# Self-attention's first query half masked by VectorE on the way out of the score banks, in a new order of work

## What is computed

```python
x = x + attn(layernorm(x))             # causal, 8 query heads of 128, 2 key/value heads from a latent of 32
x = x + xattn(layernorm(x), ctx)       # 16 heads of 16, then relu(out @ W1 + b1) @ W2 + b2
x = x + ffn(layernorm(x))              # bitlinear 256 -> 1024, gelu, bitlinear 1024 -> 256
# in attn:
scores = einsum('bqhrd,bkhd->bhrqk', q, k) * scale
scores = where(causal, scores, finfo.min)
probs = softmax(scores)
# bitlinear: rmsnorm, activations rounded to 8 bits by the row's maximum, weights rounded to -1, 0, 1
```

## Time and profile before

| | |
|---|---|
| median of 3 runs | 308.08 us (307.09 to 308.68) |
| the profiled execution | 307.61 us, of which the span from first to last instruction is 305.2 us |
| busy: PE / DVE / ACT / POOL | 287.7 / 216.4 / 236.6 / 173.7 us |
| granted TensorE clock | 1.0 throughout, the higher of its two levels (2.4 GHz) |
| DMA | 12.67 MB, nearly all in the first 40 us |

### The profile page before, as it was taken

The page is one execution under the profiler, slowest core; times in us unless marked ns, Lnnn a source line. Parts: engine busy times, 40 slices in busy tenths (PEclk is TensorE's granted clock), DMA queues, the critical chain, the costliest instruction groups (busy, mean ns, idle before and its releaser), DMA issues. The chain is left out here.

```text
span 305.2 us, 9801 instructions
## 1 busy us (share of the span) xinstructions
PE 287.7 (94%) x3502; PEld 232.1 (76%) x3502; DVE 216.4 (71%) x415; ACT 236.6 (78%) x641; POOL 173.7 (57%) x368
## 2 busy tenths in 40 slices
PE   7999798999999999999999999999999999999654
PEld 6577677788888788787888897878878968778333
DVE  1235346469787685799858586886879689799994
ACT  0668979858549759999896777997799778897672
POOL 8238225066537864055838791356825767687871
PEclk9999999999999999999999999999999999999999
DMA  7999000000000000000000010001000000000112
GB/s 210 342 366 362 31 3 1 0 2 3 2 2 3 2 3 2 3 0 2 0 4 5 2 37 0 3 1 39 1 19 3 2 3 19 30 8 3 35 34 69
DMA packets 12102, 12.67 MB, mean 42 GB/s; under 512 B 1684, under 2 KB 11288, under 8 KB 12056
## 3 DMA queue, kind: packets, MB, share of 16 engines
q1 hardware_dynamic: 10648, 11.40, 11.5%
q10 hardware_dynamic: 1408, 0.67, 0.8%
HBM read 9.96 MB, written 2.10 MB: 40 GB/s over the span
## 5 line engine op out<-in xcount | busy, mean ns | idle before, releaser
L957 ACT ACTIVATE c_p<-quad 77x512 f32<-77x512 f32 x64 | 33.3, 593 | 7.3 <-PE quad L2082 7.1
L2105 PE MATMUL bank<-c_y,xw_s 128*128 128x128 f32 x256 | 31.9, 278 | 0.7 <-DVE c_y L1493 0.7
L2105 PEld LDWEIGHTS bank<-c_y,xw_s 128*128 128x128 f32 x256 | 30.1, 192 | 1.8 <-DVE c_y L1493 0.9
L920 ACT ACTIVATE a_p<-bank 128x512 f32<-128x512 f32 x48 | 27.5, 614 | 5.0 <-PE bank L1993 5.0
L911 ACT ACTIVATE a_sB<-quad,a_nmB 128x256 f32<-128x256 f32 x64 | 29.6, 494 | 1.6 <-DVE a_nmB L1426 1.6
L2114 PE MATMUL bank<-xw_s,c_h 128*128 128x256 f32 x128 | 30.7, 384 | 0.0
L1474 DVE TENSOR_REDUCE c_nm<-quad 128x16 f32<-128x1232 f32 x16 | 22.9, 1434 | 6.1 <-PE quad L2055 5.9
L2114 PEld LDWEIGHTS bank<-xw_s,c_h 128*128 128x128 f32 x128 | 23.5, 190 | 3.9 <-issue 0.6
L1426 DVE TENSOR_REDUCE a_nmB<-quad 128x8 f32<-128x2048 f32 x8 | 18.3, 2290 | 10.6 <-PE quad L1977 10.6
L1577 DVE SCALAR_TENSOR_TENSOR f_h<-bank,f_s,fb_s 128x512 f32<-128x512 f32 x28 | 20.3, 746 | 6.8 <-PE bank L2134 6.3
L911 ACT ACTIVATE a_sA<-quad,a_nmA 128x128 f32<-128x128 f32 x64 | 22.6, 387 | 2.7 <-DVE a_nmA L1426 2.5
(11 more groups left out here) (169 smaller groups left out, 795.2 us busy)
## 6 DMA issues: line engine op xcount, KB each, us to landing
out<-f_o SPq DMA_DIRECT2D x16, 128.0 KB, 1.7
xres<-in_x SPq DMA_DIRECT2D x1, 1536.0 KB, 10.1
c_p<-in_wqT SPq DMA_DIRECT2D x2, 512.0 KB, 6.5
c_p<-in_wo SPq DMA_DIRECT2D x1, 1024.0 KB, 9.2
f_h<-in_fw1T SPq DMA_DIRECT2D x1, 1024.0 KB, 12.8
fw_t<-in_fw2T SPq DMA_DIRECT2D x1, 1024.0 KB, 11.9
xw_s<-in_xw SPq DMA_DIRECT2D x2, 512.0 KB, 10.0
fb_s<-in_fb SPq DMA_DIRECT2D x1, 512.0 KB, 6.3
```

Of the source, the lines that this page charges most:

```text
L920: nc.scalar.activation(dst, src, ACT.Copy).then_inc(sa.sem["act"], 1)
L957: nc.scalar.activation(c_p[0:M, :, qt * P:(qt + 1) * P].rearrange("p (c j g) t -> p c j g t", c=KC, g=Q2)[:, :, j, :, :], quad[0:M, j, :]. ...
L2105: last = mm(bank("xm", f"w1{t}", i)[:, m * P:(m + 1) * P], xw1_s[:, c, m * P:(m + 1) * P], c_y[:, t, c, :], start=c == 0, stop=c == KC - 1)
```

## The change

In `sa_scores` the four mask matmuls of half "A" are gone, and each of the eight score matmuls is a group of its own. A new step `sa_mask` (`sa.mkA`) on DVE reads all of half "A" out of `quad`, adds the mask (bf16, broadcast over heads) and writes the sum to a new SBUF tile `a_mA` of 128 x 1024. The reduction `sa_max` and the exponentials `sa_exp` of this half read `a_mA`. `quad` is free for its next fill once `sa_mask` is done. The lists of all engines are new, and so is the turn in which the single banks are handed out.

```diff
 QUAD_EMPTIED = {
-    ("sa", "suA"): ("act", ("exA01", "exA11", "exA21", "exA31")),
+    ("sa", "suA"): ("dve", ("mkA",)),
     ("sa", "suB"): ("act", ("exB01", "exB11", "exB21", "exB31")),
...
+MASKED_BY_VECTOR = ("A",)
...
+        a_m = {u: sb(f"a_m{u}", [P, 4, KC, P if u == "A" else T]) for u in MASKED_BY_VECTOR}
...
                 for c in range(KC):
-                    nc.scalar.activation(s[:, r, c, :], quad[:, r, c * w:(c + 1) * w], ACT.Exp, bias=nm[:, r, c:c + 1],
+                    scores = a_m[u][:, r, c, :] if u in MASKED_BY_VECTOR else quad[:, r, c * w:(c + 1) * w]
+                    nc.scalar.activation(s[:, r, c, :], scores, ACT.Exp, bias=nm[:, r, c:c + 1],
                                          accum_out=a_sum[:, qt, c, r:r + 1]).then_inc(sa.sem["act"], 1)
...
+            def sa_mask(i, u):
+
                 nm, s, w = score_tiles(u)
+                if i == 0:
+                    dve.wait_ge(ld_cst, 16 * LD_CST)
                 dve.wait_ge(*sa.after("pe", f"su{u}", i))
                 for r in range(4):
                     dve.wait_ge(*sa.after("act", f"ex{u}{r}1", i - 1))
...
+                scores = quad[:, :, 0:KC * w].rearrange("p r (c m) -> p r c m", c=KC)
...
+                nc.vector.tensor_tensor(a_m[u][:, :, :, w - P:w], scores[:, :, :, w - P:w],
+                                        mask2[:, 0:P].unsqueeze(1).unsqueeze(1).to_broadcast([P, 4, KC, P]),
+                                        op=ALU.add).then_inc(sa.sem["dve"], 1)
...
+                if u in MASKED_BY_VECTOR:
+                    scores = a_m[u][:, :, :, :]
+                    dve.wait_ge(*sa.after("dve", f"mk{u}", i))
...
                     for r in range(4):
                         rows = slice(r * L, (r + 1) * L)
-                        mm(dst[r][:, c * w:(c + 1) * w], q[rows, c, qs], k4[r][rows, 0:w], start=c == 0, stop=False)
-                for r in range(4):
+                        masked = u in MASKED_BY_VECTOR
+                        last = mm(dst[r][:, c * w:(c + 1) * w], q[rows, c, qs], k4[r][rows, 0:w], start=masked or c == 0, stop=masked)
+                for r in range(4 if u not in MASKED_BY_VECTOR else 0):
...
-        pro.v2.0 pro.k0.0 pro.k3.0 pro.v6.0 pro.wq0.0 sp.xT.0 pro.wqk0.0 pro.wq1.0 pro.v4.0 pro.wqk1.0 sp.k.0 sp.q.0
+        pro.v2.0 pro.k0.0 pro.k2.0 pro.k3.0 sp.xT.0 pro.wq0.0 pro.wq1.0 pro.wqk0.0 pro.wqk1.0 sp.k.0 sp.q.0 pro.k1.0
```

More of the change, by code:

```diff
@@ L37 @@
[L37 to L41, removed]
@@ new lines, in _ @@
+            xp_xT(1)
+            xs_exp(0, 1, 1)
+            xs_exp(0, 1, 2)
+            xs_exp(0, 1, 3)
+            xs_exp(0, 1, 0)
+            xp_q(1)
+            sa_exp(3, "A", 0)
+            sp_xT(4)
+            xs_mT(1, 0)
+            sa_exp(3, "A", 1)
+            xm_relu(0, 0)
+            sp_k(4)
+            sa_exp(3, "B", 1)
+            sa_exp(3, "B", 3)
+            sa_exp(3, "B", 2)
+            sa_exp(3, "B", 0)
+            sp_q(4)
+            xm_relu(0, 1)
+            xs_mT(1, 1)
@@ new lines, in _ @@
+            sa_tr(2, "B", 1)
+            xs_scores(0, 1)
+            sa_tr(2, "B", 0)
+            pro_v(7)
+            xs_mT(0, 0)
+            sa_tr(2, "A", 0)
+            sa_tr(2, "B", 2)
+            sa_tr(2, "B", 3)
+            sa_scores(3, "A")
+            pro_v(0)
+            xs_mT(0, 1)
+            sa_tr(2, "A", 1)
+            so_rd(2)
+            xs_shift(0, 0)
+            so_pv(2, 1)
+            pro_v(3)
+            xp_xT(1)
+            so_pv(2, 0)
+            xs_shift(0, 1)
@@ new lines, in _ @@
+            xp_q(1)
+            sp_xT(4)
+            xo_pv(0, 0)
+            xs_scores(1, 0)
+            xo_pv(0, 1)
+            so_wo(2)
+            xs_scores(1, 1)
+            xs_mT(1, 0)
+            xm_w1(0, 0)
+            sa_scores(3, "B")
+            pro_sum()
+            sp_k(4)
+            xm_w2(0, 0)
+            sp_q(4)
+            xs_mT(1, 1)
+            xm_w1(0, 1)
+            xp_xT(2)
+            xs_shift(1, 0)
+            sp_v(3)
+            xm_w2(0, 1)
+            xp_q(2)
@@ new lines, in _ @@
+            sp_q(5)
+            f1_qT(0, 0)
+            xm_w1(1, 1)
+            xs_shift(2, 1)
+            f1_l1(0, 1)
+            xm_w2(1, 1)
+            so_rd(3)
+            f1_qT(0, 1)
+            sa_scores(4, "B")
+            sp_xT(6)
+            sp_v(4)
+            so_pv(3, 1)
+            xo_pv(2, 1)
+            so_pv(3, 0)
+            f1_l1(0, 2)
+            xm_w2(1, 0)
+            f1_l1(0, 0)
+            sa_tr(4, "B", 2)
+            f1_l1(0, 3)
+            so_wo(3)
+            sa_tr(4, "B", 0)
@@ L2389, in _ @@
             so_pv(5, 1)
             xs_shift(3, 1)
+            sp_v(6)
             xs_mT(4, 0)
+            so_wo(5)
+            sp_k(7)
+            xs_shift(4, 0)
+            f2_l2(0, 0)
+            f1_qT(2, 0)
+            f2_hT(1, 1)
+            xo_pv(3, 1)
+            sa_scores(6, "A")
             xs_mT(4, 1)
-            f2_l2(0, 0)
-            so_wo(5)
-            xs_shift(4, 0)
             xm_w1(3, 0)
-            f2_l2(0, 1)
-            sa_scores(6, "A")
-            xo_pv(4, 0)
```

1672 lines of the change are left out of this document (809 added, 863 removed).

## The result

| | before | change |
|---|---|---|
| median of the runs | 308.02 us (307.09 to 308.68, 4 runs) | 303.14 us (302.58 to 303.98, 4 runs) |
| the profiled execution, its span | 307.61, 305.2 | 303.98, 302.2 |

The ratio is 0.985, with its interval 0.981 to 0.988, so the change is faster by 4.9 us; the forecast was 304.5 and 3.6 us less. The two executions therefore differ by 3.6 us only, of which 3.0 are in the span.

The account below looks back on a forecast made before the run. PE was taken to bound the kernel up to `so_wo(7)`, DVE after it. Terms -3.6, -1.8, -1.1, +1.0, +0.4 and +1.5 sum to -3.6 us: 304.0 from the profiled 307.61, plus 0.47 for the median, forecast 304.5; range 300.8 to 309.8.

Parts of the forecast that it names:

- the likeliest case: The whole kernel: the forecast's own case, faster at 304.5 us, covering 302 to 306.5; chance 0.48.
- Masks off PE: On PE: dropping four mask matmuls in each of 8 elements, at 0.45 us per element, saves 3.6 us.
- Steps that change sides of `so_wo(7)`: PE's last self-attention step: `xm_w2(5, 0)` and `xs_mT(6, 1)` go behind it, `f1_qT(4, 0)` ahead; -1.8 us.
- `quad` released earlier: In the start: PE's scores no longer wait 2.2 us for first-half exponentials; half taken, -1.1 us.
- exponentials from SBUF: On ACT in the first three elements: 37 ns more for each exponential; half taken, +0.4 us.
- DVE's list in the middle: Steps queued behind `sa_mask` on DVE make PE's 0.46 us of waits three times as long: +1.0 us.
- The end: Behind the residual of `so_wo(7)`: DVE has 1.63 us more work, of which 92% shows; +1.5 us.
- The signs: Signs of being right: 3470 matmul records, additions near 1.22 us, `so_wo(7)` near 232, then some 65 us to the last instruction.
- rival 1: In the middle: DVE sets the pace, its added work exposed and `quad` waits turned into DVE waits; 311.5 us, chance 0.17.

Follow-up runs that it names:

- the change run again: The change with no edit, timed again beside the other experiments against the kernel before: 302.75 us, ratio 0.984.
- shorter maxima: The change, with the maxima `f2_hmax` of feed-forward elements 5 to 7 taken over half of their columns: 302.24 us, ratio 0.983.
- the edit in the old order: The kernel before with its old lists, `sa_mask` put right ahead of each `sa_max(i, "A")` and `quad` released after the mask: 313.30 us, ratio 1.019.
- the old order with the narrow mask in elements 0 to 2: Old lists with `sa_mask` on DVE, its addition cut to 128 of 1024 numbers in elements 0 to 2 only: 310.11 us, ratio 1.010.
- The unmasked half A in the old order: The kernel before, with half A's four mask matmuls per element left out and nothing in their place: 305.59 us, ratio 0.994.

## Why the prediction came out right, and where not

The time, the sign and the likeliest case hold: 303.1 against 304.5 us. I go through the terms, by the profiled execution of the change run again, which is like that of before at both ends.

- **Masks off PE, -3.6.** By its runs -3.1 in the new order and -2.0 in the old one. The term is somewhat too large: counting starts gives what PE is rid of, and where PE waits for a chain anyway part of it turns into waiting. The Trainium skill's rule ("Perfetto Trace Analysis", section "Identifying the Most-Contended Engine"), read as the prediction reads it, that PE has slack at 82% of weight loads, would give about nothing. The measured 2.0 and 3.1 speak against that reading here, and the row of PE's busy time was the better guide.
- **Steps that change sides of `so_wo(7)`, -1.8.** No run has it alone. It fits the account: PE's time without work between 20 and 240 us fell from 3.60 us to 3.21 in the first execution of the change, 0.4 less; 3.1 + 1.8 + 0.4 = 5.3, and 5.3 us is what `so_wo(7)` came sooner. (The trace of the change run again lacks 13 of 3470 matmul records, so its own idle time is not used.) What is moved behind `so_wo(7)` has to be done there, so this term and that of the end belong together, and nearly cancel.
- **`quad` released earlier, -1.1**, exponentials from SBUF, +0.4, and **DVE's list in the middle, +1.0.** The waits went, all 2.2 us of them. Together the three were to add 0.3 us; PE's idle time says that they and the order took 0.4 away. The middle's +1.0 is the least secure of them and came out well: 0.65 us for 7.5 us of the addition. The exponentials in element 0 follow each other at 0.39 us with their sums, against 0.34 to 0.35 before, some 45 ns more; I had 37.
- **The end, +1.5.** 1.6 in the change run again. The size was right and its reason wrong. I reasoned that 92% of more DVE work shows because DVE is 92% busy; with shorter maxima the stretch lost 0.1 us, and with `f2_hmax(3, 1)` moved back nothing. The end is a chain over several engines, in which DVE waits little and yet isn't the bound. What in it took the 1.6 us stays open. The nearest rival is the 1.83 us of `xm_w2(5, 0)`, which PE now does there: I had it covered by PE's empty time, and no run moves it back.
- **The sum**, -3.6, was made against a profiled execution, and between the two profiled executions it is -3.6 (307.61 to 303.98). The medians differ by 4.9: before's execution lies 0.4 us below its median and the change's 0.8 above. That the two -3.6 are equal is luck. Up to `so_wo(7)` the sum had 5.1 where 5.3 came (the masks 0.5 too much, the release, the exponentials and the middle 0.7 too little), and 0.5 more came in that execution as its inputs were there earlier. The end took 2.8 in it and not 1.6, most of the difference being the wait for an output transfer. And 0.6 us came off outside the span, where I had looked for nothing: before's profiled execution has 2.4 us there, while the 54 executions of before beside the experiments have 1.9 by their median and the change has 1.8.

The signs came out as written down: 3470 records, additions of 1.22 us, no wait of the scores for exponentials of the first half, 0.5 us without work in the middle, `so_wo(7)` at 232.08. Two of them don't match the prediction's own terms: these make `so_wo(7)` 5.1 us sooner, not 5.5, and give 66.7 us from it to the last instruction (65.2 before, and 1.5), not 65. It was 66.8 in the change run again and 67.9 in the first execution, near the 68 that was to show the prediction wrong.

What I had not seen is **what the new order is for**. I treated the old order's start as a few moved steps and costed the edit's parts as if each were worth the same in any order. The runs show otherwise: the edit by itself is 5.7 us slower than before, as rival 1 describes (waits on `quad` turned into others, DVE's length exposed), only in the old order. Had the change come with the old lists, the same working without its two terms of order (-1.8 and +1.5) would have said about 305 us, and been wrong by over 8. The step that failed is the bound of DVE's term: I leant on the 44.5 us that DVE has free, and such a number doesn't tell the orders apart (41 us free in the slow one, 37 in the fast one). Rival 1's mechanism is real also in the new order, at twice the length: 5.8 of 9.8 us.

Why the new order hides the addition can be said in part. Up to 240 us PE stands idle for 5 us in the change and for 13.3 us in the old order with the edit (2.4, 6.8 and 4.0 in the three stretches), so the gain is in the main PE having other work where it would wait. The exact moves that do it were not taken apart. It is not a matter of more steps between the two fills of `quad` in element 1: by the lists these are four now (`sa_tr` three times and `so_rd`), not five as I wrote ahead of the prediction, against five before. The new order without the edit could not be tried: in five elements (1, 2, 3, 5 and 6) ACT's new list has exponentials of the second half ahead of some of the first half's, and with `quad` held until the latter the second half's scores, and so those exponentials, would wait for themselves. From the code it follows that such an order needs the early release; what that freedom is worth, beyond the 1.3 us that the release gives in the old order, no run shows.

## What to carry to other kernels

A price for an operation that moves to another engine holds only with an order of work: the same 1.22 us addition cost 0.65 us in all with one set of lists and 5.9 with another, while the busy shares of its engine in the middle were 79% and 77%. Before an engine's free time is taken as cover, follow the chain through the instruction and see whether the engine that sets the pace has other work in its list at the point where the chain comes back. And an order that has room for one load need not have room for two, as here. So try the edit in the old order, and twice the edit in the new one, before saying what either is worth.

## What the runs showed of the chip

**The clock of PE fell to its lower level behind a lull.** In the edit in the old order PE stood still for 2.13 us before 41.59 us. Windows of that kernel; the clock is the third number from the end:

```profile
39.00:42.00 3.00, 0.80 (x6) 0.38 (x5) 1.83 (x3) 3.00 (x10) 2.60 (x3) 0.99 0.01 3
42.00:45.00 3.00, 2.98 (x33) 1.80 (x34) 1.01 (x2) 0.29 (x2) 0.00 (x0) 0.50 0.00 0
45.00:48.00 3.00, 3.00 (x16) 2.72 (x16) 0.62 (x2) 2.30 (x10) 0.00 (x0) 0.95 0.00 0
```

A granted clock of 0.50 is the level of 1.2 GHz. The 32 value products that ran in it took 2.79 us; in the old order with the narrow mask in elements 0 to 2 they took 1.51 (timeline of PE):

```profile
40.33 1.51 PE L2041 MATMUL bank<-a_p,a_v 128*32 128x256 f32 x32
```

So that execution, the slowest of its kernel, paid for the wait twice: 2.13 us of it and 1.3 us behind it. It is not what sets the two kernels apart. Each has two executions with a mean granted clock of 0.999 or 1.000, of 312.5 and 312.6 us and of 309.8 and 309.9: 2.7 of the 3.2 us between the medians are there with next to no fall. The unmasked half A in the old order shows the same in its start (windows of that kernel):

```profile
34.00:36.00 2.00, 1.26 (x7) 1.26 (x8) 1.37 (x5) 2.00 (x9) 0.46 (x2) 0.76 0.00 0
36.00:38.00 2.00, 2.00 (x11) 1.78 (x9) 0.00 (x0) 2.00 (x13) 1.19 (x3) 0.50 0.00 0
38.00:40.00 2.00, 2.00 (x23) 1.29 (x22) 0.56 (x3) 1.91 (x4) 1.96 (x2) 0.89 0.00 0
```

There PE had been without work for 1.4 of the 4 us from 32 on, and then ran at the lower level for a while, which it does at no place in the profiled execution of before. It did not cost the masks their gain: six of the nine executions of this kernel have a mean granted clock of 1.000 and take 305.4 to 306.0 us, and the profiled one, with the fall, 305.5. So the clock is not why those masks were worth 2.0 us in the old order and 3.1 in the new; the reason stays open.

I had written that no term comes from the clock. That holds for the one execution that I had read. Of the 54 executions of before beside the experiments, 22 have a mean granted clock of 1.000 and a median of 307.1 us, and 20 have 0.989 and 308.1 us. Five of the nine executions of the change have 1.000, and their median is 302.6. So without any fall of the clock the change is faster by 4.5 us, and the rest of the 4.9 can be the clock. The profiled execution of the change has a fall too, near its end:

```profile
280.00:285.00 5.00, 2.10 (x14) 1.21 (x14) 4.73 (x10) 3.38 (x5) 4.12 (x12) 1.00 0.16 52
285.50:289.00 3.50, 3.33 (x17) 1.79 (x18) 3.41 (x5) 2.59 (x4) 2.38 (x6) 0.61 0.00 0
```

In the execution of the change run again the clock is 1.00 throughout the last 60 us. The stretch from the residual to the end is 66.4 us in the one and 65.2 in the other, but the clock is the smaller part of this. Up to the last instruction but one on DVE it is 63.6 and 63.4 us (297.24 and 297.52); the rest is the wait of the last one for the output transfer, 1.80 us where the other waits 0.88 for PE. Two groups of matmuls at the lower level took 1.89 and 1.88 us, where such groups take 1.04 at the higher one. But the next step began 3.39 us behind the start of the first group, and 3.06 in the other execution, where PE was done sooner and waited 1.38 us for ACT. In the old order a fall in the end went with more: the two profiled executions that have one take 64.5 and 64.8 us for that stretch, the four without 63.5 to 63.6.

**An exponential out of SBUF costs a little more than one out of PSUM.** The spacing of an exponential with its sum grew by some 45 ns in element 0. The means of the instructions alone hide this, as they overlap: 387 ns before, 407 in the change, and 388 in the edit in the old order, where the spacing is 0.38 to 0.39 us as well. The Trainium skill's page "VectorE: DVE Perf Modes", section "The TRN2 errata — SBUF-src ops pay a fixed extra latency per instruction", gives ScalarE a fixed cost of 224 cycles from SBUF and 172 from PSUM, 52 cycles at 1.2 GHz apart, by which I estimate 43 ns; the timeline agrees.
